# Splitting the late weights on GpSimd in eleven instructions, placed by waits between VectorE's operations on the maxima's parts

## The chip, the cores and the metric

One Trainium2 chip (trn2), of which the kernel uses one core. The metric is the device time of one execution in microseconds (us); lower is better. Engines are named as in the profile: PE is TensorE's matmul, PEld its weight load, DVE is VectorE, ACT ScalarE, POOL GpSimd and SP SyncE (which here issues most DMAs).

## What is computed

The reference is one block of a perceiver in float32, for a batch of 2 with 256 tokens of 256 channels and a context of 4096 keys per batch:

```python
x = x + xattn(layernorm(x), ctx, ctx, mask, ...)      # 16 heads of 16, softmax over 4096 keys
x = x + retention(layernorm(x), Wq, Wk, Wv, Wg, Wo, gnorm_w)   # 4 heads, decay, rotary, gate
x = x + experts(layernorm(x), gate_w, gate_b, expert_w, expert_b)   # 8 dense experts, softmax gate with threshold 0.1
```

The mask hides most keys; with this input the kernel finds out on the chip that the last 7 blocks of 128 keys are all it needs (the branch `fast > 0`), and every row below is of that branch.

## The kernel before

**Attention.** The work is 8 stages (`STAGES`), one for a batch and a group of 4 heads. Each stage has 7 steps (`KB`, blocks of 128 keys), so there are 56 steps (`NU`). In a step PE makes two score banks (L938), ACT takes their exponential (L1466), and PE multiplies the exponentials by the values one step later (L956). Beside that, PE makes for a coming stage eight tiles of plain scores (`max_tile`, L861), two PSUM banks each, and DVE reduces each to its row maxima (`take_maximum`, L1788). The tiles of a stage run about four steps ahead of its scores. PSUM has two pairs of banks for these tiles, so PE can be at most two tiles ahead of DVE.

**The maxima's parts.** When the eight maxima of a stage are there, `new_maximum` (L1813 to L1816) splits them into three bf16 parts in four small DVE operations: a cast into `mpart` (L1813), two subtractions (`mrest` L1814, `mpart` L1815) and a last subtraction (L1816), which signals the semaphore `max_cut`. For stages 1 to 6 this happens behind the first maximum of the next stage; for stage 7 behind its own last. So `max_cut` reaches 6 with the parts of stage 5, 7 with those of stage 6 and 8 with those of stage 7. PE then transposes the parts (`turn_rows`, L883, or `straight_rows`, L908), ACT copies them, and they ride along in the scores of that stage. All of it is in each engine's program order: what stands behind a waiting operation waits too.

**The late weights.** Retention and experts use matmuls in which each float32 factor is split into a high part (a copy, rounded to PE's float32r format) and a low part (the rest, in place of the loaded weights). SP loads the weights late: `w_ret` and others at `late_weights` (L476), the experts at `late_experts` (L491, L492). GpSimd splits them in `split_late` (L694 to L708), in eight instructions: high and low of `w_ret` (128 x 3072), of `w_gate` (128 x 16), and of each half of the experts (128 x 2048 each). It starts when `score_ready` stands at 56, half of the score banks. Behind `split_late` GpSimd has only `late_roots` (L598): eight small power operations (L596) for the normalizations; the first of them serves the second layer norm of batch 0.

**Who waits for the split.** PE waits once, in `turn_first_half` (two steps before the end of the attention), for all eight (`SPLITS` has 4 entries, two instructions each):

```python
pe.wait_ge(s["split"], 2 * len(SPLITS))
```

**The end of the attention.** From step 46 DVE normalizes batch 0's attention (`attention_tokens(0)`, L1861 and L1866, signals `at_ready` twice), adds the value bias (L1879, L1880), makes the residual stream and its layer norm (L1901, L1679, L1674), while the last steps run. Then follow retention and experts, in which PE is the busiest engine.

Of the kernel before, what the change touches and what calls it, by code (L numbers as in the profile page):

```python
# [6 lines left out]
F32 = mybir.dt.float32  # L7
# [5 lines left out]
ALU = mybir.AluOpType  # L13
# [11 lines left out]
QT = NQ // P  # L25
TT = NB * QT
KIN = D // P
# [33 lines left out]
NE = 8  # L61
# [69 lines left out]


LATE_LOADS = 7
SPLITS = ["ret", "gate", "exp0", "exp1"]


PER = {"k_ready": 8, "k_hi": 4, "k_rest": 4, "k_taken": 4, "k_mid": 4, "k_cut": 4, "v_ready": NVP + 2, "v_evac": NVP + 2,
# [100 lines left out]
def build(nc, a):  # L238
    with ExitStack() as ctx:
# [6 lines left out]
        def sb_over(of, first, name, shape):  # L246
            return nc.alloc_sbuf_tensor_at(name, shape, F32R, offset=place[of] + first)

        def sem(name):
            return ctx.enter_context(nc.semaphore(name))  # L250
# [95 lines left out]
        w_ret = w_late[:, 0:KIN * (2 * D + 2 * NV)].rearrange("p (c n) -> p c n", c=KIN)  # L346
# [15 lines left out]
        w_exp = [ctx_room[:, 0:NE * D].rearrange("p (e n) -> p e n", e=NE),  # L362
                 kpart_room[:, 0:2 * NE * D].bitcast(F32).rearrange("p (e n) -> p e n", e=NE)]

        ret_cols = KIN * (2 * D + 2 * NV)
        ret_high = sb_over("kstack", 0, "ret_high", [P, KIN, 2 * D + 2 * NV])
        ret_low = sb_over("w_late", 0, "ret_low", [P, KIN, 2 * D + 2 * NV])
        exp_high = sb_over("kstack", 4 * ret_cols, "exp_high", [P, KIN, NE, D])
        exp_low = [sb_over(of, 0, f"exp_low_{of}", [P, NE, D]) for of in ("ctxT", "kpart")]
# [31 lines left out]
        s = {n: sem(n) for n in names}  # L401
# [3 lines left out]
        only = Chunk({n: sem(n) for n in [*(n for n in PER if n not in LOOP_ONLY), *("first_k_" + n for n in ("hi", "taken", "mid", "cut"))]}, 0, False)  # L405
# [3 lines left out]
        def settle(eng):  # L409

            eng.sem_inc(s["settled"], 1)

        @contextmanager
        def each_window(eng, count):

            with eng.Fori(0, NCH) as it:
                with eng.If(it < count):
                    yield Chunk(loop_sems, it, True)
# [157 lines left out]
        def _(pool):  # L576
# [21 lines left out]
            def late_roots():  # L598
                four = QT * RH // 2
                for n, (width, first) in enumerate(((QT, 0), (QT, 0), (four, 0), (four, four), (QT, 0), (four, 0), (four, four), (QT, 0))):  # L600
                    root(NB + n, width, first)
# [16 lines left out]
            def keys_cut(c, n):  # L618
                f = n % KIN
                full = k_full[:, n % 2, :]  # L620
                pool.wait_ge(*c.key("k_taken", n))
                if c.loop:
                    settle(pool)
                if n >= 2:
                    pool.wait_ge(*c.stacked(n - 2))
                    if c.loop:
                        settle(pool)
                pool.tensor_copy(kpart[:, f, 0, :], full).then_inc(c["k_hi"], 1)
                pool.wait_ge(*c.key("k_hi", n))
                if c.loop:  # L630
                    settle(pool)
                pool.tensor_tensor(full, full, kpart[:, f, 0, :], ALU.subtract).then_inc(c["k_rest"], 1)
                pool.wait_ge(*c.key("k_rest", n))
                if c.loop:
                    settle(pool)
                pool.tensor_copy(kpart[:, f, 1, :], full).then_inc(c["k_mid"], 1)
                pool.wait_ge(*c.key("k_mid", n))
                if c.loop:
                    settle(pool)
                pool.tensor_tensor(kpart[:, f, 2, :], full, kpart[:, f, 1, :], ALU.subtract).then_inc(c["k_cut"], 1)  # L640
# [44 lines left out]
            def stream_and_bias():  # L685
                pool.wait_ge(s["w_loaded"], 16)
                pool.wait_ge(s["x_loaded"], 16)
                pool.wait_ge(s["x_second"], 16)
                pool.wait_ge(q_stacked[0], 96)
                pool.wait_ge(q_stacked[2], 96)  # L690
                for t in range(TT):
                    pool.tensor_tensor(xbo[:, t, :], x_in[:, t, :], bo_row[:, :], ALU.add).then_inc(s["xbo_ready"], 1)

            def split_late():  # L694

                pool.wait_ge(s["ret_loaded"], 16)
                pool.tensor_copy(ret_high[:, :, :], w_ret[:, :, :]).then_inc(s["split"], 1)
                pool.wait_ge(s["split"], 1)
                pool.tensor_tensor(ret_low[:, :, :], w_ret[:, :, :], ret_high[:, :, :].bitcast(F32), ALU.subtract).then_inc(s["split"], 1)
                pool.wait_ge(s["late_loaded"], 16 * LATE_LOADS)  # L700
                pool.tensor_copy(gate_high[:, :, :], w_gate[:, :, :]).then_inc(s["split"], 1)
                pool.wait_ge(s["split"], 3)
                pool.tensor_tensor(gate_low[:, :, :], w_gate[:, :, :], gate_high[:, :, :].bitcast(F32), ALU.subtract).then_inc(s["split"], 1)
                pool.wait_ge(s["experts_loaded"], 32)
                for c in range(KIN):
                    pool.tensor_copy(exp_high[:, c, :, :], w_exp[c]).then_inc(s["split"], 1)
                    pool.wait_ge(s["split"], 5 + 2 * c)
                    pool.tensor_tensor(exp_low[c][:, :, :], w_exp[c], exp_high[:, c, :, :].bitcast(F32), ALU.subtract).then_inc(s["split"], 1)  # L708

            with pool.If(fast > 0):  # L710
                pool.wait_ge(s["q_cut"], 3)

                pool.wait_ge(*only.at("max_cut", 2))
                keys_cut(only, 2)
                pool.wait_ge(*only.at("max_cut", 3))
                keys_cut(only, 3)

                pool.wait_ge(*only.at("max_cut", 4))
                stream_and_bias()

                pool.wait_ge(*only.at("score_ready", NU))
                split_late()
                late_roots()
            with pool.If(fast < 1):
                pool.wait_ge(s["q_cut"], 3)
                pool.wait_ge(*only.stacked(0))
                pool.wait_ge(*only.stacked(1))
                pool.memset(edge[0:1, :], 0.0).then_inc(s["edge_cleared"], 1)
                pool.wait_ge(s["edge_cleared"], 1)
                pool.wait_ge(s["more_ready"], 2)  # L730
                count = pool.value_load(n_windows[0:1, 0:1], min_val=1, max_val=NCH)
                pool.wait_ge(s["pad_copied"], 1)
                with each_window(pool, count) as c:
                    hide_all(c)
                    for n in range(NB * KIN):
                        keys_cut(c, n)
                    for st in range(STAGES):
                        pool.wait_ge(*c.at("alpha_ready", st + 1))
                        settle(pool)
                        pool.tensor_tensor(acc[:, st, :, :], acc[:, st, :, :],  # L740
                                           alpha[:, st % 4, :].unsqueeze(2).to_broadcast([P, TILES, E1]), ALU.mult).then_inc(c["scaled"], 1)
                    settle(pool)
                stream_and_bias()
                split_late()
                late_roots()

        @block.tensor
        def _(pe):
# [261 lines left out]
            def taken(kind, t):  # L1010

                pe.wait_ge(s["turn_taken"], TURN_AT[kind, t] + 1)
# [20 lines left out]
            def turn_xn(kind, t):  # L1033
                pe.wait_ge(s[kind + "_ready"], t + 1)
                turn(kind, t, bank[:, turn_bank(kind, t), :], xn[:, t, :], KIN)
# [17 lines left out]
            def turn_first_half():  # L1053

                pe.wait_ge(s["late_loaded"], 16 * LATE_LOADS)
                pe.wait_ge(s["split"], 2 * len(SPLITS))
                turn_xn("n2", 0)
                turn_xn("n2", 1)

# [16 lines left out]
            def tail_of_all(c):  # L1076
# [85 lines left out]
                    turn("y", t, bank[:, TB, :], y_tok[:, t, :], 4)  # L1162

                def logits(t):
                    taken("n3", t)
                    out = side("logit", t)
                    for c in range(KIN):
                        high, low = xn_high[:, c, t * P:(t + 1) * P], xn_low[:, c, t * P:(t + 1) * P]
                        pe.matmul(out[:, 0:NE], high, gate_high[:, c, :], start=(c == 0), stop=False)
                        pe.matmul(out[:, 0:NE], high, gate_low[:, c, :], start=False, stop=False)  # L1170
                        mm = pe.matmul(out[:, 0:NE], low, gate_high[:, c, :], start=False, stop=(c == KIN - 1))
                    mm.then_inc(s["side_ready"], 1)
# [973 lines left out]
```

## Time and profile before

| what | value |
|---|---|
| median of 3 runs | 223.57 us (222.64 to 225.8) |
| the profiled execution's own time | 221.97 us |
| its span in the trace | 220.1 us |
| PE busy | 202.3 us (92%) |
| DVE busy | 146.7 us (67%) |
| ACT busy | 108.4 us (49%) |
| POOL busy | 67.6 us (31%) |

The profiled execution lasts 1.87 us longer than its span, which is what lies around the traced instructions. Its own time is 1.60 us below the median of the three runs.

### The profile page before, as it was taken

How to read it: one execution, taken by the hardware profiler on the slowest of the kernel's cores; microseconds unless marked ns; L12 is line 12 of the kernel's file. 1: busy time of each engine (PE TensorE's matmuls, PEld its weight loads, DVE VectorE, ACT ScalarE, POOL GpSimd, SP SyncE). 2: the span in 40 equal slices, each digit the busy share in tenths (PEclk: the TensorE clock that was granted, in tenths of full speed). 3: DMA queues.
4: the chain of work that ended last, by engine and by line, in shares of the span. 5: the costliest groups of instructions: out<-in, count | busy, mean ns of one | idle time of the engine just before them, and what ended most of it. 6: DMA issues, size and time to landing. Idle time of an engine off the chain costs nothing.

```text
span 220.1 us, 5923 instructions
## 1 busy us (share of the span) xinstructions
PE 202.3 (92%) x2452; PEld 136.4 (62%) x2452; DVE 146.7 (67%) x291; ACT 108.4 (49%) x231; POOL 67.6 (31%) x64
## 2 busy tenths in 40 slices
PE   8898998899999999969979999989999997999990
PEld 8466654464667666625646665667888885767570
DVE  3484579985782948896898345678755526596792
ACT  2225756595783858845868973423263240211000
POOL 8317967090450500999920010010030103010000
PEclk9999999999999999996999999999999999999999
DMA  6979683354097670920000000000000000000001
GB/s 186 284 200 303 214 228 84 99 146 119 3 225 157 216 289 4 300 87 4 1 4 3 3 3 0 0 4 0 0 0 3 0 1 0 3 1 25 27 27 30
DMA packets 15794, 18.07 MB, mean 82 GB/s; under 512 B 2640, under 2 KB 14864, under 8 KB 15760
## 3 DMA queue, kind: packets, MB, share of 16 engines
q1 hardware_dynamic: 14464, 17.28, 26.8%
q10 hardware_dynamic: 1296, 0.34, 0.8%
q8 instruction: 21, 0.34, 0.6%
q14 instruction: 13, 0.11, 0.2%
HBM read 9.79 MB, written 0.52 MB: 47 GB/s over the span
## 4 chain that ended last, share of the span: by engine, by line
PE 70%; DVE 13%; DMA 4%; issue 3%; ACT 3%; SPq 3%; POOL 0%; DVEq 0%; ACTq 0%
PE bank L861 10%; PE bank L956 10%; PE bank L938 10%; DVE cneg L1788 4%; PE bank L818 4%; PE bank L804 4%; PE bank L1006 3%; PE bank L1157 3%; PE bank L1045 3%; DMA ctxT<-in_ctxT 3%; PE bank L1049 3%; PE bank L1177 3%; PE bank L1046 2%; DVE mpart L1813 2%; PE bank L1179 2%
## 5 line engine op out<-in xcount | busy, mean ns | idle before, releaser
L1788 DVE TENSOR_REDUCE cneg<-bank 128x1 f32<-128x896 f32 x64 | 67.6, 1088 | 24.8 <-PE bank L861 24.8
L1466 ACT ACTIVATE prob<-bank 128x512 f32<-128x512 f32 x112 | 64.3, 600 | 17.6 <-PE bank L938 16.3
L938 PE MATMUL bank<-qstack,kstack 100*32 100x256 bf16 x896 | 44.3, 276 | 0.9 <-ACT prob L1466 0.5
L861 PE MATMUL bank<-kstack,qstack 97*32 97x448 bf16 x512 | 37.6, 361 | 3.6 <-DVE cneg L1788 1.9
L938 PEld LDWEIGHTS bank<-qstack,kstack 100*32 100x32 bf16 x896 | 24.0, 97 | 19.8 <-ACT prob L1466 3.1
L956 PE MATMUL bank<-prob,vals 128*32 128x256 f32 x448 | 35.2, 386 | 0.0
L596 POOL TENSOR_TENSOR nw<-nw,halves 128x2 f32<-128x2 f32 (+1 forms) x10 | 8.2, 824 | 85.6 <-DVE nw L1671 59.8
L861 PEld LDWEIGHTS bank<-kstack,qstack 97*32 97x32 bf16 x512 | 12.5, 97 | 11.4 <-DVE cneg L1788 5.7
L2022 DVE SCALAR_TENSOR_TENSOR x_in<-bank,nwts,x_in 128x256 f32<-128x256 f32 x32 | 15.5, 483 | 1.1
L956 PEld LDWEIGHTS bank<-prob,vals 128*32 128x32 f32 x448 | 12.8, 110 | 4.6 <-issue 3.0
L804 PE MATMUL bank<-ctxT,wk 128*128 128x448 f32 x32 | 13.8, 555 | 0.9 <-DMA ctxT<-in_ctxT 0.9
L1177 PE MATMUL bank<-exp_high,xn_high 128*128 128x512 f32 (+1 forms) x34 | 14.4, 422 | 0.0
L818 PE MATMUL bank<-wv,ctxT 128*128 128x256 f32 x56 | 13.2, 385 | 0.0
L1179 PE MATMUL bank<-exp_high,xn_low 128*128 128x512 f32 (+1 forms) x34 | 12.9, 380 | 0.0
L818 PEld LDWEIGHTS bank<-wv,ctxT 128*128 128x128 f32 x56 | 10.3, 190 | 2.3 <-issue 1.2
L1045 PE MATMUL bank<-ret_high,xn_high 128*128 128x512 f32 x24 | 10.8, 450 | 0.7 <-ACT xn_high L1500 0.7
L1533 ACT ACTIVATE kstack<-bank 128x128 f32<-128x128 f32 x16 | 4.2, 277 | 11.0 <-PE bank L1135 11.0
L1046 PE MATMUL bank<-ret_low,xn_high 128*128 128x512 f32 x24 | 9.4, 393 | 0.0
L804 PEld LDWEIGHTS bank<-ctxT,wk 128*128 128x128 f32 x32 | 5.6, 190 | 5.4 <-issue 3.6
L1177 PEld LDWEIGHTS bank<-exp_high,xn_high 128*128 128x128 f32 x34 | 6.4, 188 | 3.1 <-DVE x_in L2022 1.5
L1049 PE MATMUL bank<-ret_high,xn_low 128*128 128x512 f32 x24 | 8.1, 398 | 0.0
L1423 ACT COPY vals<-bank 128x512 f32<-128x512 f32 (+3 forms) x6 | 3.8, 660 | 8.3 <-PE bank L818 8.3
(175 smaller groups left out, 325.4 us busy)
## 6 DMA issues: line engine op xcount, KB each, us to landing
kstack<-kpart SPq DMA_DIRECT2D x21, 224.0 KB
w_late<-in_w_ret SPq DMA_DIRECT2D x1, 1536.0 KB, 6.4
mask_all<-in_mask SPq DMA_DIRECT2D x2, 512.0 KB, 4.2
ctxT<-in_w_exp SPq DMA_DIRECT2D x1, 1024.0 KB, 5.3
kpart<-in_w_exp SPq DMA_DIRECT2D x1, 1024.0 KB, 9.1
ctxT<-in_ctxT SPq DMA_DIRECT2D x2, 448.0 KB, 5.4
ctxT<-in_ctxT SPq DMA_DIRECT2D x1, 896.0 KB, 8.0
qstack<-acc SPq DMA_DIRECT2D x12, 64.0 KB, 3.4
```

Of the source, the lines that this page charges most:

```text
L804: mm = pe.matmul(bank[:, c.key_banks(n) + h, 0:HC], wk[:, i, f * P:(f + 1) * P], ctxT[:, b, i, h * HC:(h + 1) * HC], start=(i == 0), stop= ...
L818: mm = pe.matmul(out[:, (k - blocks[0]) * D:(k - blocks[0] + 1) * D], ctxT[:, b, i, k * P:(k + 1) * P], wv[:, i, :], start=(i == 0), stop= ...
L861: mm = pe.matmul(out[j4:j4 + COLS, :], qstack[0:MROW + 1, h, b, qt * P + j4:qt * P + j4 + COLS], kstack[0:MROW + 1, b, h, half_ * HC:(half ...
L938: mm = pe.matmul(out[j4:j4 + COLS, hh * NQ:(hh + 1) * NQ], kstack[0:KROWS, b, h, kt * P + j4:kt * P + j4 + COLS], qstack[0:KROWS, h, b, :] ...
L956: mm = pe.matmul(bank[32 * j:32 * j + PADV, OB, 0:NQ], vals[:, b, kt, e:e + PADV], prob[:, (2 * u + j // 2) % PROBS, (j % 2) * NQ:(j % 2 + ...
L1045: pe.matmul(bank[:, 2 + m, :], xn_high[:, c, t * P:(t + 1) * P], ret_high[:, c, cols], start=(c == 0), stop=False)
L1049: mm = pe.matmul(bank[:, 2 + m, :], xn_low[:, c, t * P:(t + 1) * P], ret_high[:, c, cols], start=False, stop=(c == KIN - 1))
L1177: pe.matmul(out, high, exp_high[:, c, experts, :], start=(c == 0), stop=False, skip_group_check=True)
L1179: return pe.matmul(out, low, exp_high[:, c, experts, :], start=False, stop=(c == KIN - 1), skip_group_check=True)
L1466: act.activation(prob[:, n % PROBS, :], bank[:, c.score_bank(u, jj), :], ACT.Exp).then_inc(c["prob_ready"], 1)
L1788: dve.tensor_reduce(cneg[:, st % 2, i:i + 1], bank[:, pair:pair + 2, 0:HC], AXXY, ALU.max, negate=True).then_inc(c["max_read"], 1)
L2022: dve.scalar_tensor_tensor(x_in[:, t, :], src, nwts[:, t, e:e + 1], x_in[:, t, :], ALU.mult, ALU.add).then_inc(s["pair_read"], 1)
```

## The change

GpSimd's split is made of eleven instructions: the high parts are as before, the low part of `w_ret` is written in two halves (one for each 1536 columns), and each expert half's low part in two (1024 columns each). Between them stand three waits, `after(0)`, `after(1)` and `after(2)`: for `max_cut` at 6, for `max_cut` at 7, and for `at_ready` at 2. PE's wait in `turn_first_half` asks for the first three instructions (all of `w_ret`) and a wait for all eleven stands in `logits`, where the gate's and the experts' weights are first used. The branch not taken here gets no waits. The diff, cut to its core:

```diff
-SPLITS = ["ret", "gate", "exp0", "exp1"]
+SPLIT_RET = 3
+SPLIT_EXPERT = (6, 9)
+SPLIT_ALL = 11
...
-            def split_late():
+            def split_late(after):
 
                 pool.wait_ge(s["ret_loaded"], 16)
                 pool.tensor_copy(ret_high[:, :, :], w_ret[:, :, :]).then_inc(s["split"], 1)
                 pool.wait_ge(s["split"], 1)
-                pool.tensor_tensor(ret_low[:, :, :], w_ret[:, :, :], ret_high[:, :, :].bitcast(F32), ALU.subtract).then_inc(s["split"], 1)
+
+                def ret_rest(c):
+                    pool.tensor_tensor(ret_low[:, c, :], w_ret[:, c, :], ret_high[:, c, :].bitcast(F32), ALU.subtract).then_inc(s["split"], 1)
+
+                def exp_whole(c):
+                    pool.tensor_copy(exp_high[:, c, :, :], w_exp[c]).then_inc(s["split"], 1)
+                    pool.wait_ge(s["split"], SPLIT_EXPERT[c])
+
+                def exp_rest(c, i):
+                    some = slice(i * NE // 2, (i + 1) * NE // 2)
+                    pool.tensor_tensor(exp_low[c][:, some, :], w_exp[c][:, some, :], exp_high[:, c, some, :].bitcast(F32), ALU.subtract
+                                       ).then_inc(s["split"], 1)
+
+                ret_rest(0)
+                after(0)
+                ret_rest(1)
                 pool.wait_ge(s["late_loaded"], 16 * LATE_LOADS)
                 pool.tensor_copy(gate_high[:, :, :], w_gate[:, :, :]).then_inc(s["split"], 1)
-                pool.wait_ge(s["split"], 3)
+                pool.wait_ge(s["split"], SPLIT_RET + 1)
                 pool.tensor_tensor(gate_low[:, :, :], w_gate[:, :, :], gate_high[:, :, :].bitcast(F32), ALU.subtract).then_inc(s["split"], 1)
                 pool.wait_ge(s["experts_loaded"], 32)
-                for c in range(KIN):
-                    pool.tensor_copy(exp_high[:, c, :, :], w_exp[c]).then_inc(s["split"], 1)
-                    pool.wait_ge(s["split"], 5 + 2 * c)
-                    pool.tensor_tensor(exp_low[c][:, :, :], w_exp[c], exp_high[:, c, :, :].bitcast(F32), ALU.subtract).then_inc(s["split"], 1)
+                exp_whole(0)
+                exp_rest(0, 0)
+                after(1)
+                exp_rest(0, 1)
+                exp_whole(1)
+                exp_rest(1, 0)
+                after(2)
+                exp_rest(1, 1)
+
+            def between_cuts(i):
+
+                if i < 2:
+                    pool.wait_ge(*only.at("max_cut", 6 + i))
+                else:
+                    pool.wait_ge(s["at_ready"], QT)
...
                 pool.wait_ge(*only.at("score_ready", NU))
-                split_late()
+                split_late(between_cuts)
                 late_roots()
...
             def turn_first_half():
 
                 pe.wait_ge(s["late_loaded"], 16 * LATE_LOADS)
-                pe.wait_ge(s["split"], 2 * len(SPLITS))
+                pe.wait_ge(s["split"], SPLIT_RET)
...
                 def logits(t):
+                    pe.wait_ge(s["split"], SPLIT_ALL)
                     taken("n3", t)
```

## Rows read from the trace of the kernel before

**Rows 1.** The page: busy time of the engines, and the granted clock in 40 slices.
```profile
PE 202.3 (92%) x2452; PEld 136.4 (62%) x2452; DVE 146.7 (67%) x291; ACT 108.4 (49%) x231; POOL 67.6 (31%) x64
...
PEclk9999999999999999996999999999999999999999
```

**Rows 2.** Timeline of DVE, 84 to 125 us (start, us, engine, line, op).
```profile
84.59 0.16 DVE L1813 CAST mpart<-cneg 128x8 bf16<-128x8 f32 x1
...
85.06 0.17 DVE L1816 TENSOR_TENSOR mpart<-mrest,mpart 128x8 bf16<-128x8 f32 x1
...
91.67 0.30 DVE L1834 COPY acc<-bank 128x136 f32<-128x136 f32 x1
92.40 1.09 DVE L1788 TENSOR_REDUCE cneg<-bank 128x1 f32<-128x896 f32 x1 [0.43 <-PE bank L861]
...
94.66 3.34 DVE L1813 CAST mpart<-cneg 128x8 bf16<-128x8 f32 x1
...
98.32 0.17 DVE L1816 TENSOR_TENSOR mpart<-mrest,mpart 128x8 bf16<-128x8 f32 x1
...
109.58 1.81 DVE L1813 CAST mpart<-cneg 128x8 bf16<-128x8 f32 x1
...
119.04 1.09 DVE L1788 TENSOR_REDUCE cneg<-bank 128x1 f32<-128x896 f32 x1 [0.43 <-PE bank L861]
120.17 0.17 DVE L1813 CAST mpart<-cneg 128x8 bf16<-128x8 f32 x1
...
121.12 0.76 DVE L1866 TENSOR_TENSOR vals<-acc,rsum 128x256 f32<-128x256 f32 x2
123.43 0.35 DVE L1879 TENSOR_SCALAR xnT<-bank,bv 128x128 f32<-128x128 f32 x1 [1.55 <-PE bank L1006]
```

**Rows 3.** Timeline of POOL from 84 us on.
```profile
88.41 2.75 POOL L697 CAST ret_high<-w_late 128x3072 fp32r<-128x3072 f32 x1 [13.66 <-PE bank L938]
91.24 6.74 POOL L699 TENSOR_TENSOR ret_low<-w_late,ret_high 128x3072 fp32r<-128x3072 f32 x1
97.92 0.20 POOL L701 CAST gate_high<-w_gate 128x16 fp32r<-128x16 f32 x1
98.20 0.22 POOL L703 TENSOR_TENSOR gate_low<-w_gate,gate_high 128x16 fp32r<-128x16 f32 x1
98.36 1.89 POOL L706 CAST exp_high<-ctxT 128x2048 fp32r<-128x2048 f32 x1
100.33 4.54 POOL L708 TENSOR_TENSOR exp_low_ctxT<-ctxT,exp_high 128x2048 fp32r<-128x2048 f32 x1
...
106.79 4.57 POOL L708 TENSOR_TENSOR exp_low_kpart<-kpart,exp_high 128x2048 fp32r<-128x2048 f32 x1
130.62 0.71 POOL L596 TENSOR_TENSOR nw<-nw,halves 128x2 f32<-128x2 f32 x1 [19.26 <-DVE nw L1671]
```

**Rows 4.** Engines in stretches: from one cast of L1813 to the next.
```profile
core 0: us, PE busy (x) PEld busy (x) DVE busy (x) ACT busy (x) POOL busy (x), PEclk, DMA share, GB/s
94.66:109.58 14.92, 12.25 (x244) 7.11 (x236) 12.34 (x14) 8.68 (x16) 14.68 (x7) 0.89 0.03 8
109.58:120.17 10.59, 9.05 (x216) 5.42 (x212) 9.73 (x14) 7.74 (x15) 1.78 (x1) 1.00 0.02 5
84.59:94.66 10.07, 10.05 (x244) 6.35 (x236) 9.09 (x14) 8.60 (x16) 6.17 (x2) 1.00 0.62 203
```

**Rows 5.** Timeline of PE, 98 to 104 us.
```profile
98.54 0.22 PE L883 MATMUL bank<-identb,mpart 128*16 128x128 bf16 x1 [1.27 <-DVE mpart L1816]
...
99.54 0.56 PE L861 MATMUL bank<-kstack,qstack 97*32 97x448 bf16 x8 [0.50 <-DVE cneg L1788]
...
100.88 0.97 PE L861 MATMUL bank<-kstack,qstack 97*32 97x448 bf16 x8
```

**Rows 6.** Groups of POOL by form: the nearest smaller subtraction.
```profile
L632 POOL TENSOR_TENSOR k_full<-k_full,kpart 128x896 f32<-128x896 f32 x3 | 5.7, 1893 | 0.2
```

**Rows 7.** The page's DMA issues (KB each, median us from issue to landing).
```profile
ctxT<-in_w_exp SPq DMA_DIRECT2D x1, 1024.0 KB, 5.3
kpart<-in_w_exp SPq DMA_DIRECT2D x1, 1024.0 KB, 9.1
```

**Rows 8.** Timeline of SP: the second of the experts' loads is issued.
```profile
87.74 0.58 SPq L492 DMA_DIRECT2D kpart<-in_w_exp  x1
```

**Rows 9.** The instructions of the gate's logits, the first use of the split experts and gate.
```profile
L1171 PE MATMUL bank<-gate_high,xn_low x8: 252/253/253, 177.9 to 202.2; 128*128 128x8 f32 x8
```

More of the change, by code:

```diff
@@ L743, in _ @@
                 stream_and_bias()
-                split_late()
+                split_late(lambda i: None)
                 late_roots()
```

## The prediction

> **What bounds the kernel now.** I read the page first, then the chain of waits, and then DVE, POOL and PE in order of time around the place where the split runs. The page gives PE 92% of the span [rows 1], so a gain must come from stretches in which PE is idle or slow. Its clock row has one dent, in slice 19 of 40 (about 99 to 104.5 us), and that is where the split runs. In the timeline of DVE the reader is to look at the casts of L1813, one for each stage, 8 elements wide. An ordinary one takes 0.16 us. The one at 94.66 takes 3.34 us and the one at 109.58 takes 1.81 us [rows 2]. Nothing in their shape differs, but in POOL's timeline the subtraction into ret_low runs from 91.24 to 97.98, and that into exp_low_kpart from 106.79 to 111.36 [rows 3]. The casts end at 98.00 and 111.39, within 0.03 us of those ends. So a cast that is issued while a long GpSimd subtraction runs stands until that is over. Of the eight casts only these two meet such an instruction. I take this as a block of the whole instruction, and the change as one that takes both meetings away.
>
> DVE's other work goes on beside GpSimd: the copy from PSUM at 91.67 takes 0.30 us in the middle of ret_low, and a reduction at 92.40 takes its usual 1.09 us [rows 2].
>
> What the stalls cost PE is read in the stretches from cast to cast [rows 4]. 84.59 to 94.66 is an undisturbed stage: 10.07 us, PE busy for 10.05 of it with 244 matmuls. The next stage, the same 244 matmuls, takes 14.92 us: PE is busy for 12.25 and idle for 2.67. Part of the busy time is a lower clock: the mean granted clock of that stretch is 0.89, and an eight of L861 takes 0.97 us at 100.88 where it took 0.56 at 99.54 [rows 4, 5]. The low stretch follows the idle time, in which PE waited for the parts and then for a maximum (1.27 and 0.50 us) [rows 5].
>
> **The change part by part, against the profiled execution.** First what goes.
>
> First stall, with all that follows from it: 14.92 - 10.07 = 4.85 us [rows 4]. Of this 3.34 - 0.16 = 3.18 us is the stall, and 1.67 us is the low clock and what PE could not make good.
>
> Second stall: from the cast at 109.58 to the last reduction of stage 7 at 119.04 are 9.46 us; in the undisturbed stage the same seven tiles take from 84.59 to 92.40, 7.81 us [rows 2]. The difference is 1.65 us, the stall itself (1.81 - 0.16). The clock was 1.00 there [rows 4], so nothing is added.
>
> Together 4.85 + 1.65 = 6.50 us.
>
> Now whether the new placing avoids the casts. Nothing ahead of the first cast changes, so it stays at 94.66. GpSimd's high copy of w_ret ends at 91.16 and the first half starts at 91.24. Its duration is not in the trace. Half of 6.74 is 3.37 us; a straight line between 1.893 us for 896 columns [rows 6] and 4.54 us for 2048 [rows 3] gives 1.89 + 640 x 0.00230 = 3.36 us. I take 3.37, so it ends at 94.61, 0.05 us ahead of the cast. That is thin, but it costs little if it fails: each 0.1 us that it is late holds the cast by as much. The bounds are no stall and 0.4 us (a half of 3.8 us, twice the 896-column row).
>
> The wait for max_cut at 6 ends with the parts' last operation, 0.64 us after the cast starts (84.59 to 85.23 [rows 2]), so at 95.30. Behind it: second half 3.37 to 98.75; the gate's two instructions 0.44 (97.92 to 98.36 [rows 3]) to 99.2; the copy of the first experts 1.97 with its gap (98.36 to 100.33) to 101.2; half of their subtraction, 2.19 us by the same line for 1024 columns, to 103.4. The experts have landed: the second load is issued at 87.74 and takes 9.1 us [rows 7, 8], to 96.8. The second cast comes one undisturbed stage after the first, at 94.66 + 10.07 = 104.73. Margin 1.3 us.
>
> The wait for max_cut at 7 ends at 105.37. Then 2.19 + 0.08 + 1.89 + 0.08 + 2.19 give 111.8. The third cast follows at 8.94 us in an undisturbed stage (7.81 to the last reduction and 120.17 - 119.04 = 1.13 behind it [rows 2]), at 113.67. Margin 1.9 us.
>
> The wait for at_ready ends with L1866, at 121.88 - 6.50 = 115.38; the last half runs to 117.6. DVE's next operation is L1879 at 123.43 - 6.50 = 116.93, which reads PSUM. Its like beside a GpSimd subtraction is the copy from PSUM of 0.30 us [rows 2], so I take no cost; the other end is 0.7 us, if it waited for the half's end.
>
> The Trainium skill, page "SBUF — State Buffer", section "Who interferes with whom", says that VectorE and GpSimd share a port pair as an exclusive lock for a whole instruction, and counts a VectorE operation with two SBUF inputs among those that meet a GpSimd read. For the casts the trace agrees (the end within 0.03 us). For the two-input operations it shows no block: L1816 at 98.32 took 0.17 us beside gate_low, which ran to 98.42, though that is a small instruction. By the page those three operations would be held too if GpSimd ran on right after the cast; by the row they would not; the sum stays the same, since the waits are for the fourth.
>
> What is queued behind the waits on GpSimd is only its own split and the roots. The first root is at 130.62 [rows 3], moved to 124.1, 6.5 us after the split's new end at 117.6. PE's wait for w_ret asks for the third instruction, at 98.75, and its transposes follow the layer norm behind that first root, 25 us later. The wait in logits asks for the eleventh, at 117.6, and is reached at 177.9 less 6.5 [rows 9]. Three more GpSimd instructions add a gap each, 0.08 us (91.16 to 91.24 [rows 3]), on an engine that has the room. All this I cost at nothing on the path; its cover is these margins.
>
> Is something else late next? In the undisturbed stage PE is busy for 10.05 of 10.07 us, DVE for 9.09, ACT for 8.60 [rows 4], so PE sets the pace and 10.07 us is what a stage can be. Behind step 46 all is chained to PE's progress and no load is under way, so the 6.50 us reach the end whole.
>
> The sum: 221.97 - 6.50 = 215.5 us for the profiled execution. Its own time is 1.60 us below the median of the three runs. Against the median: 223.57 - 6.50 = 217.07, so I predict 217.1 us.
>
> **The rivals.**
> (a) *The clock dips anyway.* The stalls go, but PE's low stretch comes at some other time, as the runs of before spread over 3 us without a difference in the program. Only the stalls are gained: 3.18 + 1.65 = 4.83 us, 218.7 us. For it: PE is idle for 17.8 us of the span [rows 1], of which the two disturbed stretches hold 4.2 [rows 4]. Against it: the clock row shows no second dent in 220 us [rows 1].
> (b) *A half still meets a cast.* The first is 0.05 us clear by the rows, the second 1.3. If the first cast waits for 0.4 us the time is 217.5. If the second also met exp_low's half, the most is a hold of 2.2 us, with a clock that may fall: 6.50 - 2.6 = 3.9 us gained, 219.7 us.
> (c) *The change does not do what it says:* the casts are long for another reason (a wait on something that only looks like GpSimd's end). Then the time stays, 223.6 us. Against it stand two ends that agree within 0.03 us and six short casts.
> (d) *Slower.* The last half hangs on at_ready, and in GpSimd's order the first root stands behind it. If the split got so late that this root waited, DVE's layer norm and with it PE would stand, and PE's clock would fall as behind the first stall, which made 4.85 us out of 3.18. It decides only from a point where the split ends 6.5 us later than worked out; to eat the whole gain, the root must be late by about 6.50 x 3.18 / 4.85 = 4.3 us more, so the split late by 10.8 us. With a split late by 13 us the loss would be (13 - 6.5) x 4.85 / 3.18 = 9.9 us and the time 223.57 - 6.50 + 9.9 = 227 us. Nothing in the rows holds GpSimd for so long.
>
> **How the numbers follow.** The forecast 0.70, (a) 0.15, (b) 0.10 (most of it in its small form), (c) 0.03, (d) 0.02. The forecast's own spread is that of a median of three runs, some 1.5 us to each side, since those of before span 222.64 to 225.8. The range is 214.8 to 220.2 us: below, the profiled sum 215.5 less 0.7 for runs as quick as that one; above, the dear form of (b) and 0.5. A measurement of this kernel can tell about 2% (4.5 us) from no change. Under 219.1 us lie most of the forecast, most of (a) and the small form of (b): faster 0.82. Within 2%: 0.15, from (c), the dear form of (b) and the tails of the others. Slower: 0.03.
>
> **What would show it.** In the changed profile all eight casts of L1813 take 0.16 to 0.17 us (the one at 94.66 perhaps up to 0.5). From cast to cast the last two stretches are about 10.1 and 8.9 us in place of 14.92 and 10.59, PE idle in them under 0.2 us, and the granted clock is 1.00 throughout. GpSimd has three gaps that end with mpart L1816 twice and vals L1866 once; its split ends near 117.6. The first root comes near 124.1, the logits' last matmul near 195.7, and the span is about 213.6 us. The forecast is wrong if a cast is still over 1 us long, if a stage without a long cast still takes over 11 us (then PE's loss had another source), if the clock row has a dent elsewhere, or if the stages are short and the tail longer than before.

## The result and the profile after

The changed kernel takes 216.57 us (median of 4, 215.62 to 217.18), the kernel before beside it 223.1 us (median of 4). The ratio is 0.9723 with a 95% interval of 0.9653 to 0.9793: faster, by 6.5 us of these medians. An execution that took over 1.5% more than its kernel's fastest is left out of every ratio, here the 225.8 us of before; without it the kernel before has 222.64 us and the gain is 6.1 us. The forecast was 217.1. The profiled execution's own time is 217.18 us, its span 215.3 us.

The page's busy times and clock row, as [rows 1]:

```profile
PE 199.7 (93%) x2452; PEld 135.2 (63%) x2452; DVE 142.2 (66%) x291; ACT 108.2 (50%) x231; POOL 68.2 (32%) x67
...
PEclk9999999999999999999999999999999999999999
```

The dent in the clock row is gone. Next the timeline of DVE, as [rows 2]; the changed file is longer, so the cast is L1842, the last of the four operations L1845 and the reduction L1817.

```profile
85.72 0.16 DVE L1842 CAST mpart<-cneg 128x8 bf16<-128x8 f32 x1
...
95.81 0.16 DVE L1842 CAST mpart<-cneg 128x8 bf16<-128x8 f32 x1
...
106.97 0.16 DVE L1842 CAST mpart<-cneg 128x8 bf16<-128x8 f32 x1
...
115.91 0.17 DVE L1842 CAST mpart<-cneg 128x8 bf16<-128x8 f32 x1
...
119.17 0.35 DVE L1908 TENSOR_SCALAR xnT<-bank,bv 128x128 f32<-128x128 f32 x1 [1.55 <-PE bank L1034]
```

Every cast takes 0.16 or 0.17 us, where two took 3.34 and 1.81. The timeline of POOL, as [rows 3]:

```profile
89.54 2.75 POOL L699 CAST ret_high<-w_late 128x3072 fp32r<-128x3072 f32 x1 [14.22 <-PE bank L966]
92.37 3.49 POOL L703 TENSOR_TENSOR ret_low<-w_late,ret_high 128x1536 fp32r<-128x1536 f32 x1
96.53 3.47 POOL L703 TENSOR_TENSOR ret_low<-w_late,ret_high 128x1536 fp32r<-128x1536 f32 x1 [0.67 <-DVE mpart L1845]
...
102.36 2.38 POOL L711 TENSOR_TENSOR exp_low_ctxT<-ctxT,exp_high 128x1024 fp32r<-128x1024 f32 x1
107.69 2.38 POOL L711 TENSOR_TENSOR exp_low_ctxT<-ctxT,exp_high 128x1024 fp32r<-128x1024 f32 x1 [2.96 <-DVE mpart L1845]
...
117.70 2.36 POOL L711 TENSOR_TENSOR exp_low_kpart<-kpart,exp_high 128x1024 fp32r<-128x1024 f32 x1 [3.34 <-DVE vals L1895]
126.37 0.71 POOL L598 TENSOR_TENSOR nw<-nw,halves 128x2 f32<-128x2 f32 x1 [6.31 <-DVE nw L1700]
```

The three waits show as the gaps of 0.67, 2.96 and 3.34 us, each with its releaser. The first root comes after 6.31 us of idle time, so it still has that much to spare. The stretches from cast to cast, as [rows 4]:

```profile
85.72:95.81 10.09, 10.07 (x244) 6.22 (x236) 9.09 (x14) 8.62 (x16) 6.18 (x2) 1.00 0.65 205
95.81:106.97 11.16, 10.28 (x244) 6.59 (x236) 9.36 (x15) 8.49 (x16) 8.09 (x6) 1.00 0.03 9
106.97:115.91 8.94, 8.87 (x216) 5.48 (x212) 8.09 (x14) 7.66 (x15) 6.58 (x3) 1.00 0.02 5
```

10.59 us became 8.94, the 8.94 that the prediction worked out. But 14.92 became 11.16 and not 10.07. The timeline of PE shows where the rest lies:

```profile
95.95 0.36 PE L889 MATMUL bank<-kstack,qstack 97*32 97x448 bf16 x1
97.19 0.56 PE L889 MATMUL bank<-kstack,qstack 97*32 97x448 bf16 x7 [0.88 <-issue]
```

In the middle of a group of eight matmuls PE is idle for 0.88 us without a releaser. The kernel before had the same gap at the same place of its program:

```profile
94.80 0.36 PE L861 MATMUL bank<-kstack,qstack 97*32 97x448 bf16 x1
96.06 0.56 PE L861 MATMUL bank<-kstack,qstack 97*32 97x448 bf16 x7 [0.90 <-issue]
```

There it lay inside the first stall and cost nothing: behind it PE waited only 1.27 us more for the parts [rows 5], together 2.17 us.

The account between the two profiled executions: from the cast at 84.59 (85.72 after) to the one at 120.17 (115.91 after), 35.58 us became 30.19, a gain of 5.39. Ahead of it the changed execution is 1.13 us later, in a part of the program that was not changed (in two further profiles of the changed kernel, shown below, this cast starts at 85.17 and 84.28); behind it, 99.93 us became 99.39. Together 5.39 - 1.13 + 0.54 = 4.80, the difference of the spans.

### The profile page after: what moved, and what is told of

Read it like the earlier page. It is cut to its first block, busy times and chain, and to the rows that moved or that the text cites. A ratio compares the mean times of both kernels' runs of the same rounds, so it can differ in the third digit from the quotient of the medians.

```text
span 215.3 us, 5926 instructions
## 1 busy us (share of the span) xinstructions
PE 199.7 (93%) x2452; PEld 135.2 (63%) x2452; DVE 142.2 (66%) x291; ACT 108.2 (50%) x231; POOL 68.2 (32%) x67
## 4 chain that ended last, share of the span: by engine, by line
PE 74%; DVE 9%; DMA 5%; ACT 4%; SPq 3%; issue 3%; POOL 0%; DVEq 0%; ACTq 0%
PE bank L889 11%; PE bank L984 11%; PE bank L966 11%; PE bank L846 4%; PE bank L832 4%; DVE cneg L1817 3%; PE bank L1034 3%; PE bank L1185 3%; DMA ctxT<-in_ctxT 3%; PE bank L1073 3%; PE bank L1206 3%; PE bank L1077 3%; PE bank L1074 2%; PE bank L1208 2%; PE bank L1207 2%
## 5 line engine op out<-in xcount | busy, mean ns | idle before, releaser
L1817 DVE TENSOR_REDUCE cneg<-bank 128x1 f32<-128x896 f32 x64 | 67.8, 1088 | 24.5 <-PE bank L889 24.4
L966 PE MATMUL bank<-qstack,kstack 100*32 100x256 bf16 x896 | 43.8, 273 | 1.5 <-ACT prob L1495 1.1
L889 PE MATMUL bank<-kstack,qstack 97*32 97x448 bf16 x512 | 36.9, 354 | 2.6 <-issue 0.9
```

The lines of the kernel that those rows point to most:

```text
L889: mm = pe.matmul(out[j4:j4 + COLS, :], qstack[0:MROW + 1, h, b, qt * P + j4:qt * P + j4 + COLS], kstack[0:MROW + 1, b, h, half_ * HC:(half ...
L966: mm = pe.matmul(out[j4:j4 + COLS, hh * NQ:(hh + 1) * NQ], kstack[0:KROWS, b, h, kt * P + j4:kt * P + j4 + COLS], qstack[0:KROWS, h, b, :] ...
L1817: dve.tensor_reduce(cneg[:, st % 2, i:i + 1], bank[:, pair:pair + 2, 0:HC], AXXY, ALU.max, negate=True).then_inc(c["max_read"], 1)
```

## The experiments

Four asked what holds the small operations, two what each wait is worth, one what late weights cost, and the rest PE's gap. They ran in three series, each beside the kernel before on the same chip; its medians there were 222.77, 223.31 and 222.56 us.

### The split without the waits

```diff
-                split_late(between_cuts)
+                split_late(lambda i: None)
```

> The eleven instructions without the three waits. Theory A (a cast that is issued while a GpSimd instruction runs stands until that instruction ends): GpSimd goes on without a gap. With the high copy's end taken as 0 the halves of w_ret run from 0.08 to 3.57 and from 3.6 to 7.0, and the first cast is issued 3.5 us after it: either it comes between the two (0.16 us long) or it meets the second half (up to 3.4 us long); the second cast meets the copy or the half subtraction of the second experts and is held by up to 2.4 us. Total between the changed kernel and the one before, 217 to 222 us. Rival B (the casts were long by the length of the instruction alone, so halving is enough): both casts under 0.5 us and 216.6 us.

Measured: 222.92 us, ratio 1.0031 (0.9995 to 1.0066). The split into eleven instructions alone is worth nothing that can be measured, and the time is above the 217 to 222 us that were expected. The timeline of DVE at the two casts:

```profile
94.75 3.50 DVE L1842 CAST mpart<-cneg 128x8 bf16<-128x8 f32 x1
...
111.06 0.87 DVE L1842 CAST mpart<-cneg 128x8 bf16<-128x8 f32 x1
```

The timeline of POOL, the two halves merged:

```profile
91.33 6.89 POOL L703 TENSOR_TENSOR ret_low<-w_late,ret_high 128x1536 fp32r<-128x1536 f32 x2
```

The two halves stand back to back and end at 98.22; the cast, issued where the one ends and the other begins, is held for the whole of the second, to 98.25. That is theory A's worse case. The second cast is held for the end of the last half. Rival B falls. From the first cast to the second are 16.31 us with a mean granted clock of 0.79, against 14.92 us with 0.89 in the kernel before, though the first cast is held only 0.16 us longer. That eats up what the second cast gains, which takes 0.87 us and not 1.81.

### The waits without the halves

The subtraction of w_ret in one piece behind `after(0)`, and for each half of the experts the high copy, the wait, and the subtraction in one piece (the counts in `SPLIT_RET`, `SPLIT_EXPERT` and `SPLIT_ALL` follow; lines left out are marked):

```diff
-                ret_rest(0)
                 after(0)
-                ret_rest(1)
+                pool.tensor_tensor(ret_low[:, :, :], w_ret[:, :, :], ret_high[:, :, :].bitcast(F32), ALU.subtract).then_inc(s["split"], 1)
...
+                for c in range(KIN):
+                    exp_whole(c)
+                    after(1 + c)
+                    pool.tensor_tensor(exp_low[c][:, :, :], w_exp[c], exp_high[:, c, :, :].bitcast(F32), ALU.subtract).then_inc(s["split"], 1)
```

> The eight whole instructions of before with the three waits: the subtraction of w_ret behind max_cut at 6, that of the first experts behind max_cut at 7, that of the second behind at_ready. Theory A: no instruction runs while a cast is issued, all eight casts 0.16 us, 216.6 us, the same as the changed kernel; GpSimd's split ends about 5 us later than there, still ahead of the first root, by about 2 to 4 us. Rival B (short instructions are what helps): a cast of over 1 us and over 218 us.

Measured: 215.7 us, ratio 0.9669 (0.962 to 0.9718); all casts short. Its POOL timeline:

```profile
95.32 6.78 POOL L715 TENSOR_TENSOR ret_low<-w_late,ret_high 128x3072 fp32r<-128x3072 f32 x1 [4.29 <-DVE mpart L1840]
```

The whole 6.78 us fit between two casts, since they are 10.36 us apart there. So the waits are what the change is worth, and the halves add nothing that can be measured; a third series below has both forms on one chip.

### Another operation in the cast's place

```diff
-                link(c, dve.tensor_copy(mp[:, :, 1, :], mv))
+                link(c, dve.tensor_reduce(mp[:, :, 1, :], mv.unsqueeze(3), AXX, ALU.max))
```

> The kernel before, with one edit: the cast of the maxima into bf16 is written as a maximum over an axis of one element, so that it is another kind of operation with the same result. GpSimd's split is untouched. Theory A with the page's list (a reduction does not meet GpSimd, an operation with two SBUF inputs does): the first part takes 0.2 us, but the subtraction behind it (mrest) is held for the rest of the GpSimd subtraction, 3.2 and 1.6 us: time as before, 223 us. Rival C (only the cast needs the shared port; the two-input operations do not meet GpSimd): all four parts short at both places, the first stall and the second gone without any change to GpSimd: 216.6 us. Rival D (any small operation on SBUF is held): the reduction itself lasts 3.3 and 1.8 us, 223 us.

Measured: 222.46 us, ratio 0.9974 (0.9937 to 1.001). The profiled execution took 225.38 us, the longest of its ten, so only the lengths of single operations are read from it. DVE at the two places:

```profile
94.66 0.15 DVE L1813 TENSOR_REDUCE mpart<-cneg 128x8 bf16<-128x8 f32 x1
94.85 3.15 DVE L1814 TENSOR_TENSOR mrest<-cneg,mpart 128x8 f32<-128x8 f32 x1
...
107.76 0.15 DVE L1813 TENSOR_REDUCE mpart<-cneg 128x8 bf16<-128x8 f32 x1
107.95 3.43 DVE L1814 TENSOR_TENSOR mrest<-cneg,mpart 128x8 f32<-128x8 f32 x1
```

The reduction passes beside GpSimd's long subtraction in 0.15 us, and the two-input subtraction behind it is held until GpSimd's ends (98.0 and 111.4). C and D fall. This is the division that the Trainium skill gives, page "SBUF — State Buffer", section "Who interferes with whom": a reduction (`tensor_reduce`) never contends with GpSimd on this chip, a copy or cast can, in a mode that uses both ports, and an operation with two inputs from SBUF contends with a GpSimd instruction that reads SBUF. The traces agree: 3.34 and 1.81 us for the casts of before, 0.15 us for the reduction, 3.15 and 3.43 us for the operation with two inputs.

### GpSimd goes on right after the cast

```diff
-                    pool.wait_ge(*only.at("max_cut", 6 + i))
+                    pool.wait_ge(*only.at("dve_chain", 3 * (5 + i) + 1))
```

> The changed kernel, but the first two waits end with the cast (the first of the four operations on the parts) and not with the fourth, so GpSimd's half subtraction starts while the three two-input subtractions are still to come. Theory A with the page's rule: one of the three is held for 3.4 us at the first place and for 2.3 us at the second, and the kernel takes 216.6 + 5 = about 221 to 222 us. Rival C (the two-input operations do not meet GpSimd): all stay at 0.17 us and the time stays at 216.6 us.

Measured: 229.4 us (225.91 to 230.69), ratio 1.0208 (1.0102 to 1.0314): slower than the kernel before, from a wait that ends three small operations early; whether by over 2% the interval leaves open. DVE at the two places:

```profile
94.91 0.17 DVE L1843 TENSOR_TENSOR mrest<-cneg,mpart 128x8 f32<-128x8 f32 x1
94.99 3.43 DVE L1844 TENSOR_TENSOR mpart<-cneg,mpart 128x8 bf16<-128x8 f32 x1
...
111.33 2.35 DVE L1844 TENSOR_TENSOR mpart<-cneg,mpart 128x8 bf16<-128x8 f32 x1
113.72 1.79 DVE L1845 TENSOR_TENSOR mpart<-mrest,mpart 128x8 bf16<-128x8 f32 x1
```

At the second place two operations are held one after the other, L1844 by the half subtraction and L1845 by the copy that follows it. The expectation (221 to 222 us) counted one hold there and no clock, and was 7 to 8 us short. The mean granted clock is 0.962 to 0.973 in the four executions, against 0.975 to 0.992 in those of the kernel before beside them.

### The first stall kept

```diff
-                ret_rest(0)
-                after(0)
-                ret_rest(1)
+                pool.tensor_tensor(ret_low[:, :, :], w_ret[:, :, :], ret_high[:, :, :].bitcast(F32), ALU.subtract).then_inc(s["split"], 1)
```

> The changed kernel, but the subtraction of w_ret stays one instruction right behind its copy, with no wait at the first place; the rest is as changed. Theory A: the first cast is held for 3.2 us as before, the second is short. The first stall is worth what the profiles of before and after give, 14.92 - 11.16 = 3.8 us, so 220.3 us; by the prediction's 4.85 it would be 221.4 us.

Measured: 219.45 us, ratio 0.9835 (0.9774 to 0.9895): faster than the kernel before, though the interval leaves open whether by 2%, and 3.75 us over the changed kernel on the same chip (215.7). Expected were 220.3 or 221.4. The stretches of its profile, in which the first cast takes 3.35 us:

```profile
95.72:108.98 13.26, 10.59 (x244) 6.38 (x236) 12.28 (x15) 8.68 (x16) 7.89 (x5) 1.00 0.03 8
108.98:117.92 8.94, 8.87 (x216) 5.42 (x212) 8.08 (x13) 7.66 (x15) 6.60 (x3) 1.00 0.02 5
```

Here the clock stayed at 1.00, and the stage is 13.26 - 10.07 = 3.19 us too long, just the stall. So the slow stretch behind the first stall does not come in every execution; of the four here three had a mean granted clock of 0.992 to 1.0 and one 0.977, with 223.05 us.

Between the medians on this chip the two stalls come out otherwise than between the profiles: with the second gone and the first kept, 223.31 became 219.45, 3.86 us; with both gone, 3.75 us more. The second is dearer than its 1.65 us in the profile. That fits the clock, since in the 17 executions of the kernel before beside it only 3 had 0.992; with four executions of this kernel it is not shown.

### The second wait dropped

```diff
                 exp_rest(0, 0)
-                after(1)
                 exp_rest(0, 1)
```

> The changed kernel without the wait for max_cut at 7; the other two stay. By the changed kernel's profile the second half of the first experts would then run from 4.8 to 7.2 us after the start of the gate's copy (from 104.7 to 107.1 on its time axis), and the second cast is issued at 106.97 there, or about a microsecond earlier in an execution without PE's gap. Theory A: the cast is held for the rest of that half, 0.1 to 1.3 us, and the time is 0 to 1.5 us over the changed kernel's (216 to 217.5 us). If this wait were needless in every execution: no cast over 0.2 us and the same time.

Measured: 222.29 us, ratio 1.0004 (0.9964 to 1.0044). One dropped wait gives back the whole gain, where 1.5 us at most was expected. The timeline of DVE at the second cast:

```profile
104.78 1.24 DVE L1841 CAST mpart<-cneg 128x8 bf16<-128x8 f32 x1
106.06 1.79 DVE L1842 TENSOR_TENSOR mrest<-cneg,mpart 128x8 f32<-128x8 f32 x1
107.77 0.15 DVE L1843 TENSOR_TENSOR mpart<-cneg,mpart 128x8 bf16<-128x8 f32 x1
107.96 2.31 DVE L1844 TENSOR_TENSOR mpart<-mrest,mpart 128x8 bf16<-128x8 f32 x1
```

The timeline of POOL beside it:

```profile
101.27 4.72 POOL L711 TENSOR_TENSOR exp_low_ctxT<-ctxT,exp_high 128x1024 fp32r<-128x1024 f32 x2
105.93 1.89 POOL L706 CAST exp_high<-kpart 128x2048 fp32r<-128x2048 f32 x1
107.91 2.34 POOL L711 TENSOR_TENSOR exp_low_kpart<-kpart,exp_high 128x1024 fp32r<-128x1024 f32 x1
```

The engines in the stretch from this cast to the next (columns as in [rows 4]):

```profile
104.78:120.78 16.00, 11.57 (x216) 6.38 (x212) 13.09 (x13) 7.84 (x15) 5.38 (x3) 0.79 0.01 3
```

Each hold ends with a GpSimd instruction (105.99, 107.82, 110.25), and by then the next GpSimd instruction is ahead of the next small operation; only L1843 passes, in 0.15 us. A series of four small operations meets a series of GpSimd instructions and loses to three of them: 1.24 + 1.79 + 2.31 less three times 0.17 is 4.8 us. PE is idle for 4.19 us, then the clock is low: 16.00 us for what takes 8.94.

### The experts' split late

All six of the experts' instructions behind `after(2)`.

```diff
+                after(2)
                 exp_whole(0)
                 exp_rest(0, 0)
-                after(1)
                 exp_rest(0, 1)
                 exp_whole(1)
                 exp_rest(1, 0)
-                after(2)
                 exp_rest(1, 1)
```

> All six instructions of the experts' split are put behind the wait for at_ready, so that nothing of them stands between the casts, and GpSimd reaches the first root late: they take 13.6 us from 117.7 on (by the durations in the changed kernel's profile), to 131.3, where the root is wanted at 126.4. This prices the prediction's slower rival. If the lateness goes to the end one to one: 216.6 + 4.9 = 221.5 us. With a slower clock behind PE's idle time, as in the first stall (4.85 out of 3.18): up to 224 us. If there is slack behind the root: under 220 us.

Measured: 222.27 us, ratio 0.9967 (0.9925 to 1.0009), 6.6 us over the changed kernel on the same chip. The timeline of POOL at the first root:

```profile
128.79 0.70 POOL L598 TENSOR_TENSOR nw<-nw,halves 128x2 f32<-128x2 f32 x1
```

The timeline of DVE, from the variance to the normalization that needs the root:

```profile
123.95 0.17 DVE L1699 TENSOR_SCALAR nw<-moments 128x2 f32<-128x2 f32 x1
129.60 0.73 DVE L1702 TENSOR_SCALAR xn<-mask_all,moments,nw 128x256 f32<-128x256 f32 x2 [5.48 <-POOL nw L598]
```

The timeline of PE, the first transposes behind it:

```profile
130.27 1.09 PE L1033 MATMUL bank<-ident,xn 128*128 128x128 f32 x4 [4.65 <-DVE xn L1702]
```

The variance is there at 124.12; in the changed kernel the root follows such an end by 0.08 us, so here it is 4.6 us late. PE waits for 4.65 us, and 6.6 us of the whole time are lost: 1.43 for each microsecond of lateness, inside the 221.5 to 224 us that were expected.

### PE's gap: the second experts' load later

`second_experts` is the load of `w_exp[1]` with a semaphore of its own, for which GpSimd waits ahead of `exp_whole(1)`.

```diff
                 late_experts()
-                for st in range(5, STAGES - 1):
-                    load_rows(only, st)
+                load_rows(only, 5)
+                second_experts()
+                load_rows(only, 6)
...
```

> The changed kernel with one more edit: the load of the second experts (1 MB) is issued behind the maxima rows of stage 5, some 10 us later, and GpSimd waits for it ahead of their high copy. PE's gap of 0.88 us without a releaser, in the middle of a group of L889 in the stage of the first cast, is what is asked. Theory E (PE's instructions are fetched late because the experts' load fills the DMA engines just then): the gap is gone, that stage is 10.1 us in place of 11.16, and the median is lower by up to 1 us. Rival F (the gap belongs to that place of PE's program): the gap stays and the time is that of the changed kernel.

> The changed kernel again, unedited, beside the others on the same chip: 216.6 us. Its profile tells whether PE's gap of 0.88 us comes in every execution of the same program (rival F) or only in some (theory E, by how the load and the fetch meet).

Measured on one chip: 215.29 us (0.9642, 0.9604 to 0.9681) with the later load, 215.7 us (0.9659, 0.9616 to 0.9702) for the changed kernel. The engines in the stretch behind the first cast, with the later load:

```profile
94.84:104.91 10.07, 10.05 (x244) 6.28 (x236) 9.09 (x14) 8.61 (x16) 8.13 (x6) 1.00 0.34 108
```

The same stretch of the changed kernel, second profile:

```profile
95.27:105.59 10.32, 10.26 (x244) 6.59 (x236) 9.16 (x14) 8.50 (x16) 8.11 (x6) 1.00 0.05 14
```

The same program that had the gap of 0.88 us shows none of that size here, but a smaller lateness at the same place. The group of eight with the later load, then in two further profiles of the changed kernel (this one and the third):

```profile
94.97 0.56 PE L894 MATMUL bank<-kstack,qstack 97*32 97x448 bf16 x8
...
95.40 0.98 PE L889 MATMUL bank<-kstack,qstack 97*32 97x448 bf16 x8
...
94.49 1.00 PE L889 MATMUL bank<-kstack,qstack 97*32 97x448 bf16 x8
```

Both were run once more, with the whole-instruction form beside them:

> The changed kernel with the later second load, again, beside the changed kernel on the same chip. Theory E: again no gap, stage of the first cast 10.1 us, all executions within 1.1 us of each other as the six before (214.53 to 215.55), median 215.3 us. Rival F: a gap of 0.9 us in the profile or a spread like the changed kernel's (3 us).

> The changed kernel for the third time: 215.7 to 216.6 us with a spread of some 3 us. Under theory E its profile shows a stage of the first cast of over 10.1 us in most executions (11.16 and 10.32 us in the two so far).

> Eight whole instructions with the three waits, and the load of the second experts behind the maxima rows of stage 5: the simplest form of the change with the later load. Theory A and E: all casts 0.16 us, no gap of PE without a releaser, 215.3 us, as with halves. If halves matter after all: over 216.5 us.

Measured: 216.06 us (0.9712, 0.9658 to 0.9766; 214.65 to 217.51) with the later load, 216.11 us (0.9724, 0.9673 to 0.9774) for the changed kernel, 215.64 us (0.9707, 0.9653 to 0.976) for whole instructions with the later load. The stretch is 10.07 or 10.08 us in all three profiles with the later load, and 11.16, 10.32 and 10.36 in three of the changed kernel. But two other kernels with the early load had 10.09 and 10.08 there (the experts' split late, and the second wait dropped). The group of eight separates the two better than the stretch: it takes 0.56 us in all three profiles with the later load, and 0.73 to 1.02 us in eight with the early load, among them these two (0.73 each), and 1.80 and 1.82 us with the gaps of 0.88 and 0.90 (GpSimd going on after the cast has a third such gap, 0.94 us). So rival F, a lateness that belongs to the place alone, falls: it comes with the early load only, and costs up to 1.1 us of the stage. (The same edit puts the rows of stage 5 ahead of that load; the two were not tested apart.) How the load makes PE late, by a delayed fetch of instructions as theory E has it or otherwise, no run shows.

None of this is seen in the whole time. The narrow spread of the first series did not come again (2.9 us in place of 1.0 with the later load, which was rival F's sign), and no median differs by more than the runs of one kernel do. The three forms take the same time.

## Why the prediction was right

**What is removed.** That GpSimd's long instructions hold the casts is shown from four sides: with the waits alone the casts are short, with the split alone they are not, a reduction in the cast's place passes, and a wait that ends early moves the hold to the next operation.

**The second stall, 1.65 us.** Right for the pair: 10.59 became 8.94. Between medians it was worth more, 3.86 us, by the run with the first stall kept.

**The first stall, 4.85 us.** Right in kind; in the profiled pair it came to 3.76 us (14.92 - 11.16), because PE's gap, hidden by the stall before, is on the path after. In the profiles with the later load the stage is 10.07 or 10.08 us, and in two with the early load 10.08 and 10.09; there the term is the full 4.85. That the stall covered PE's lateness shows in the wait for the parts: 1.27 us behind the gap of 0.90, but 2.07 us with the first stall kept, where the group of eight took 1.02 us in one piece. The gap was in the trace of before, ahead of PE's wait for the parts, and the prediction passed over it: its step "so PE sets the pace and 10.07 us is what a stage can be" took another stage's time for this one's.

**The signs.** By its own list the prediction was wrong on one point in the profiled execution: a stage without a long cast was not to take over 11 us, and this one took 11.16. What it placed in time came 2.2 to 2.5 us later than it said, for the most part by the 1.13 us ahead of that stage and the 1.09 us in it: the split's end at 120.06 (said: 117.6), the first root at 126.37 (124.1), the logits' last matmul at 197.9 (195.7). The span was 215.3 us and not 213.6. In the third profile of the changed kernel, where this stage took 10.36 us, the span is 213.2.

**Why the median still agreed.** The sum took the clock's loss from one execution, whose mean granted clock was 0.992. In the three series of experiments the kernel before ran 53 times beside them: 11 executions had 0.989 or 0.992 and a median of 221.5 us, 42 had 0.985 or less and 223.1 us (222.9 without the six longest). What such an execution can look like is seen in the profile of the split without waits, at 0.979: 16.31 us where the profile of before has 14.92. In 16 executions of the changed kernel 13 had 0.992 or more. So before, a typical execution lost more to the low clock than the profiled one. The medians differ by 6.5 us and the two profiled executions by 4.79: that of before was 1.13 us below its median, and that of the changed kernel, the longest of its four, 0.61 us above. The forecast's 6.50 was too large for the pair that it was worked out on and about right for the medians; in part that is luck. Rival (a), that the clock would dip anyway, has a small true core: 3 of these 16 had 0.985 to 0.988 and took 216.59 to 217.98 us, the three at 0.999 or 1.0 beside them 214.93 to 215.64. In the second profile of the changed kernel (217.71 us, mean granted clock 0.992) the clock row has the dent elsewhere that the prediction named as a sign of being wrong; from 180 to 188 us the granted clock was 0.77 and 0.80:

```profile
PEclk9999999999999999999999999999999998899999
```

**The times of the halves.** 3.37 was taken, 3.49 measured; 2.19 taken, 2.38 measured. The first half's record ends at 95.86 and the cast starts at 95.81, not held. So by the records the margin of 0.05 us was gone, and the cast was short even so. The held casts of before ended 0.02 and 0.03 us behind GpSimd's records, less than the 0.16 us that a cast takes, so DVE seems to be let go a little before such a record ends. The cast was short in every profile of this placing; the split without waits shows what it costs when another GpSimd instruction stands right behind.

**The slack.** No cost, as forecast: the roots had 6.31 us, L1908 took its 0.35 us beside the last half, the logits' first use of the split weights came at 173.4 us, 53 us behind the eleventh instruction.

**Where a reading failed.** The prediction set the rule of the Trainium skill on operations with two inputs (page "SBUF — State Buffer", section "Who interferes with whom") against a row, L1816 with 0.17 us beside gate_low, and read it as "no block". The runs show the rule right (3.15, 3.43, 2.35 us) and the row too weak: gate_low is 0.22 us long, so the row could not tell the two apart. The wrong reading changed nothing in the sum, as the waits are for the fourth operation. But rival (b) was priced with "the most is a hold of 2.2 us", and the run without the second wait shows what that meeting costs, 6 us and more. The margin of 1.3 us that the prediction worked out for the second cast was the right thing to look at, but its loss would have cost the whole gain, not 2.2 us.

**The slower rival (d).** Its price for a late root, 4.85 / 3.18 = 1.53 for each microsecond, stands beside the measured 1.43.

## What to carry to other kernels

Read VectorE's smallest operations one by one: a cast of 8 elements that takes 3 us is no long cast but a held one, and its end on the end of a GpSimd instruction says by whom. Place long GpSimd work by waits on the last of VectorE's small operations, not on the first, and check by its durations that it is over before the next group; cutting it into shorter pieces without waits helped nothing here. What a stall hides (here a gap of PE of 0.9 us) is to be taken off its price, and the clock's loss behind a stall is to be taken from more executions than the profiled one.

## What the runs showed that was not expected

A series of short operations, a cast and the two-input subtractions behind it, loses to one GpSimd instruction after another: three holds of 1.24, 1.79 and 2.31 us from one cast that came 1.2 us too early. The loss that follows is larger than the holds: 16.00 us for a stretch of 8.94, with a mean granted clock of 0.79, after PE had been idle for 4.19 us; behind the idle time the eights of L888 took 0.94 and 0.97 us in place of 0.55, and from 116.05 on they took 0.55 again (timeline of PE, second wait dropped):

```profile
111.32 0.94 PE L888 MATMUL bank<-kstack,qstack 97*32 97x448 bf16 x8 [0.19 <-DVE cneg L1816]
...
113.75 0.97 PE L888 MATMUL bank<-kstack,qstack 97*32 97x448 bf16 x8
...
116.05 0.55 PE L888 MATMUL bank<-kstack,qstack 97*32 97x448 bf16 x8
```

And a stall does not fix its own price: a hold of 3.2 to 3.3 us of the first cast cost 4.85 us in the profiled execution of before, 6.24 us (16.31 - 10.07) in that of the split without waits, and 3.19 us in that with the first stall kept, where the clock stayed at 1.00. What decides between these, no run shows.
